# Three accumulator banks, one side bank, and a quarter of each unit's gram parts moved from ScalarE to VectorE

## What is computed

```
dots = jnp.einsum('bfd,bgd->bfg', bottom_output, bottom_output)
x = concatenate([bottom_mlp_output, dots[:, _TRIL_I, _TRIL_J], pad], axis=1)
for w, b in ((w0, b0), (w1, b1), (w2, b2), (w3, b3)):      # 480-1024-1024-512-256
    x = relu(x @ w.T + b)
return x @ w_out.T + b_out
```

## Time and profile before

| | |
|---|---|
| median of 3 runs | 526.17 us (526.14 to 526.34) |
| the profiled execution | 524.71 us, of which the span of instructions is 522.9 us |
| granted TensorE clock over the span | 0.994 |
| TensorE busy | 496.2 us, 95% of the span |
| ScalarE, VectorE, GpSimd busy | 333.8, 289.3, 258.4 us |

### The profile page before, as it was taken

The page is one execution under the profiler, slowest core; times in us unless marked ns, Lnnn a source line. Parts: engine busy times, 40 slices in busy tenths (PEclk is TensorE's granted clock), DMA queues, the critical chain, the costliest instruction groups (busy, mean ns, idle before and its releaser), DMA issues.

```text
span 522.9 us, 13445 instructions
## 1 busy us (share of the span) xinstructions
PE 496.2 (95%) x4073; PEld 485.5 (93%) x4073; DVE 289.3 (55%) x644; ACT 333.8 (64%) x846; POOL 258.4 (49%) x467
## 2 busy tenths in 40 slices
PE   6987988899999999999999999999999999999996
PEld 6976977899999899999999999999999999999996
DVE  2775767476762676357753676356743686231101
ACT  3665788667884698657883698557873798423112
POOL 2710354425774287625764287525763386524221
PEclk9989999999999999999999999999999999999999
DMA  8988877654663666266653657256643762210000
GB/s 229 237 288 169 259 115 121 126 100 72 100 98 69 114 104 107 45 122 112 102 80 78 118 97 112 54 117 106 97 74 88 123 98 37 64 34 1 1 1 0
DMA packets 281054, 53.23 MB, mean 102 GB/s; under 512 B 265126, under 2 KB 279230, under 8 KB 281022
## 3 DMA queue, kind: packets, MB, share of 16 engines
q1 hardware_dynamic: 279090, 52.22, 52.9%
q10 hardware_dynamic: 1932, 0.61, 0.5%
HBM read 45.71 MB, written 7.09 MB: 101 GB/s over the span
## 4 chain that ended last, share of the span: by engine, by line
PE 74%; DMA 7%; ACT 4%; issue 4%; SPq 4%; POOL 3%; DVE 2%; ACTq 0%; POOLq 0%; DVEq 0%
PE acc L732 60%; PE gram_ps L694 7%; DMA rows<-in_r_bottom_output_dram 3%; PE gram_ps L646 2%; DMA early_rows<-in_r_bottom_output_dram 2%; PE gram_ps L675 2%; ACT parts L823 2%; DMA blocks<-grams 2%; SPq L462 2%; ACT h_full L839 1%; SPq L414 1%; POOL parts L568 1%; POOL h_a L583 1%; POOL grams L575 1%; PE turned_ps L651 1%
## 5 line engine op out<-in xcount | busy, mean ns | idle before, releaser
L732 PE MATMUL acc<-h_a,w_hi 128*128 128x256 f32 x1152 | 223.5, 285 | 3.1 <-ACT h_full L839 2.8
L732 PEld LDWEIGHTS acc<-h_a,w_hi 128*128 128x128 f32 x1152 | 184.7, 191 | 5.7 <-ACT h_full L839 3.8
L823 ACT ACTIVATE parts<-gram_ps 27x216 f32<-27x216 f32 x448 | 152.9, 341 | 24.5 <-PE gram_ps L694 14.6
L839 ACT ACTIVATE h_full<-acc,small_t 128x256 f32<-128x256 f32 x172 | 81.4, 473 | 128.9 <-PE acc L732 125.9
L732 PE MATMUL acc<-h_a,w_lo 128*128 128x256 f32 x576 | 158.7, 282 | 0.0
L583 POOL TENSOR_TENSOR h_a<-h_full,h_a 128x256 fp32r<-128x256 f32 x96 | 72.3, 753 | 138.4 <-DVE h_a L956 138.4
L732 PEld LDWEIGHTS acc<-h_a,w_lo 128*128 128x128 f32 x576 | 110.2, 191 | 0.0
L732 PE MATMUL acc<-h_b,w_hi 128*128 128x256 f32 x512 | 97.4, 285 | 0.0
L732 PE MATMUL acc<-x,w_hi 128*128 128x256 f32 x480 | 95.1, 287 | 2.4 <-ACT h_full L839 1.3
L925 DVE STREAM_TRANSPOSE raw<-rows 128x512 f32<-128x512 f32 x112 | 78.7, 703 | 11.6 <-DMA rows<-in_r_bottom_output_dram 11.6
L583 POOL TENSOR_TENSOR h_b<-h_full,h_b 128x256 fp32r<-128x256 f32 x64 | 47.3, 739 | 74.6 <-DVE h_b L956 74.6
(11 more groups left out here) (59 smaller groups left out, 437.9 us busy)
## 6 DMA issues: line engine op xcount, KB each, us to landing
rows<-in_r_bottom_output_dram SPq DMA_DIRECT2D x444, 64.0 KB, 2.0
blocks<-grams SPq DMA_DIRECT2D x30, 216.0 KB, 4.0
w_raw<-in_L_rec_w_dram SPq DMA_DIRECT2D x6, 1024.0 KB, 7.9
early_rows<-in_r_bottom_output_dram SPq DMA_DIRECT2D x12, 224.0 KB, 6.3
stage_pairs<-in_L_rec_w_dram SPq DMA_DIRECT2D x1, 1408.0 KB, 10.2
w_raw<-in_L_rec_w_dram SPq DMA_DIRECT2D x2, 512.0 KB, 9.6
mlp_rows<-r_bottom_mlp_output_dram SPq DMA_DIRECT2D x8, 128.0 KB, 2.2
pairs<-blocks SPq DMA_DIRECT2D x8, 126.0 KB
```

The costliest lines, as they stand in the source:

```text
L732: last = nc.tensor.matmul(acc_slot(c, slot), weight(wp, layer, m, k), in_tile(layer, k, xp), start=(k == 0 and n == 0), stop=(k == K_TILES ...
L823: last = nc.scalar.activation(parts[quad_of(s), u % 2, :, :, 0:FEATS], gram_found(u, s), ACT.Copy)
L839: nc.scalar.activation(h_full[:, slot % 2, :], acc_slot(c, slot), ACT.Relu, bias=small_t[:, slot:slot + 1]).then_inc(drained, 1)
```

## The change

There are now three accumulators (`RING_OF`: slot modulo 3, but slot 21 goes to bank 1), one side bank `side_ps` and the four of `gram_ps`. The side bank holds the dense input in columns 0 to 255 and the output row in the others; the rows turned at the start use it and accumulator 2 in turn. `slot_before` finds the slot whose drain a slot waits for. Only four tiles get their first input early, so W1's groups have all four banks of `gram_ps`. Of each unit's four quads ScalarE copies three, and VectorE the fourth (`gram_parts_rest`), as its last instruction of a hook; TensorE's next use of the banks, VectorE's transposition and GpSimd's sum wait for both.

```
-ACC_RING, TURN_RING, GRAM_RING = 2, 2, 2
+ACC_RING, GRAM_RING, TURN_RING = 3, 2, 2
+RING_OF = [n % 3 for n in range(SLOTS - 1)] + [1]
+QUADS_BY_ACT = 3
-OUT_HOOK, EARLY_TILES = 2, 6
+OUT_HOOK, EARLY_TILES = 2, 4
+def slot_before(slot, first):
+    def bank(of):
+        return ACC_RING if first and of == ACC_RING else RING_OF[of % SLOTS]
+    for of in range(slot - 1, -1 if first else slot - 1 - SLOTS, -1):
+        if bank(of) == bank(slot):
+            return of
+    return None
...
-            among = EARLY_TILES // 3 if BEFORE_CHUNK <= n < LATE_WEIGHTS else GRAM_RING * GRAM_BANKS
-            return gram_ps[:, n % among, :]
+            return gram_ps[:, n % (GRAM_RING * GRAM_BANKS), :]
...
                 pool.wait_ge(parts_done, n)
+                pool.wait_ge(parts_rest_done, n)
...
-                elif BEFORE_CHUNK <= n < LATE_WEIGHTS:
-                    pe.wait_ge(w_done, max(n - 1, BEFORE_CHUNK))
...
                     pe.wait_ge(parts_done, (d - 1) * UNITS + u + 1 - GRAM_RING)
+                    pe.wait_ge(parts_rest_done, (d - 1) * UNITS + u + 1 - GRAM_RING)
...
-                        of = slot - EARLY_TILES if isinstance(c, int) and c == 0 and slot < M_TILES[0] else slot - ACC_RING
+                    of = slot_before(slot, isinstance(c, int) and c == 0)
+                    if of is not None:
                         pe.wait_ge(drained, slot_count(c, of))
...
-                for s in range(GROUP):
+                for s in range(QUADS_BY_ACT):
                     last = nc.scalar.activation(parts[quad_of(s), u % 2, :, :, 0:FEATS], gram_found(u, s), ACT.Copy)
...
+            def gram_parts_rest(d, u):
+                dve.wait_ge(gram_done, d * UNITS + u + 1)
...
+                    dve.wait_ge(grams_done, d * UNITS + u - 1)
+                for s in range(QUADS_BY_ACT, GROUP):
+                    last = nc.vector.tensor_copy(parts[quad_of(s), u % 2, :, :, 0:FEATS], gram_found(u, s))
+                last.then_inc(parts_rest_done, 1)
...
                 dve.wait_ge(parts_done, n)
+                dve.wait_ge(parts_rest_done, n)
```

More of the change, by code:

```diff
@@ L52 @@
 LAST_LAYER = [(0, 0, 3, HIGH), (1, 0, 3, HIGH), (0, 3, 4, HIGH), (1, 3, 4, HIGH), (0, 0, 4, LOW), (1, 0, 4, LOW)]
-ACC_RING, TURN_RING, GRAM_RING = 2, 2, 2
+ACC_RING, GRAM_RING, TURN_RING = 3, 2, 2
 GRAM_BANKS = 2
 XT_RING, XT_LAG = 4, 2
-assert ACC_RING + TURN_RING + GRAM_RING * GRAM_BANKS == 8 and SLOTS % ACC_RING == 0
+assert ACC_RING + 1 + GRAM_RING * GRAM_BANKS == 8
+RING_OF = [n % 3 for n in range(SLOTS - 1)] + [1]
 HOOK, FIRST_HOOK = 18, 6
@@ L274, in dlrm_program @@
         acc = ctx.enter_context(nc.psum_tensor("acc", [P, ACC_RING, 512], F32))
-        turned_ps = ctx.enter_context(nc.psum_tensor("turned_ps", [P, TURN_RING, 512], F32))
+        side_ps = ctx.enter_context(nc.psum_tensor("side_ps", [P, 512], F32))
         gram_ps = ctx.enter_context(nc.psum_tensor("gram_ps", [P, GRAM_RING * GRAM_BANKS, 512], F32))
@@ L302, in dlrm_program @@
         parts_done = sem("parts_done")
+        parts_rest_done = sem("parts_rest_done")
         low_turned = sem("low_turned")
@@ L343, in acc_slot, with turned_bank @@
         def acc_slot(c, slot):
[L344 to L351, removed]
+            if isinstance(c, int) and c == 0 and slot == ACC_RING:
+                return side_ps[:, 0:CHUNK]
+            return acc[:, RING_OF[slot], 0:CHUNK]
+        def turned_bank(u):
+            return side_ps if u % TURN_RING else acc[:, ACC_RING - 1]
+        mlp_bank = side_ps[:, 0:CHUNK]
+        out_bank = side_ps[0:1, CHUNK:]
         def in_tile(layer, k, part):
@@ L392, in turned_cols @@
         def turned_cols(u):
-            return turned_ps[:, u % TURN_RING, 0:UNIT_COLS].rearrange("p (j s f) -> p j s f", s=GROUP, f=FEATS)
+            return turned_bank(u)[:, 0:UNIT_COLS].rearrange("p (j s f) -> p j s f", s=GROUP, f=FEATS)
         def quad_of(s):
@@ L619, in turn_weights @@
                     pe.wait_ge(parts_done, UNITS)
+                    pe.wait_ge(parts_rest_done, UNITS)
                 elif n >= LATE_WEIGHTS + ring:
@@ L650, in turn_rows @@
                 for j in range(UNIT_GROUPS):
-                    last = nc.tensor.transpose(turned_ps[:, u % TURN_RING, j * GROUP_ROWS:(j + 1) * GROUP_ROWS],
+                    last = nc.tensor.transpose(turned_bank(u)[:, j * GROUP_ROWS:(j + 1) * GROUP_ROWS],
                                                src[0:GROUP_ROWS, j, :], ident[0:GROUP_ROWS, 0:GROUP_ROWS])
@@ L715, in products @@
                         pe.wait_ge(w_done, W0_GROUPS if layer == 0 and m >= 4 else groups_for(layer, m))
-                    if not (isinstance(c, int) and c == 0 and slot < EARLY_TILES):
-                        of = slot - EARLY_TILES if isinstance(c, int) and c == 0 and slot < M_TILES[0] else slot - ACC_RING
+                    of = slot_before(slot, isinstance(c, int) and c == 0)
+                    if of is not None:
                         pe.wait_ge(drained, slot_count(c, of))
@@ L940, in early_rest @@
                 last.then_inc(grams_done, 1)
+            def gram_parts_rest(d, u):
+                dve.wait_ge(gram_done, d * UNITS + u + 1)
+                if isinstance(d, int) and d == 1 and u < 2:
+                    dve.wait_ge(parts_zeroed, 1)
+                else:
+                    dve.wait_ge(grams_done, d * UNITS + u - 1)
+                for s in range(QUADS_BY_ACT, GROUP):
+                    last = nc.vector.tensor_copy(parts[quad_of(s), u % 2, :, :, 0:FEATS], gram_found(u, s))
+                last.then_inc(parts_rest_done, 1)
             def turn_low(d, u):
@@ L999, in chunk @@
                         turned_lo(c + step[1], step[2])
+                    elif step[0] == "gram":
+                        gram_parts_rest(c + step[1], step[2])
                     elif step[0] == "sum":
```

## The result

The changed kernel takes 518.76 us in the median of 5 runs (517.22 to 520.58), the kernel before 526.24 beside it. The ratio is 0.9868, 95% interval 0.9846 to 0.989: faster by 6.9 us, 5.8 to 8.1. The profiled execution took 517.22 us (span 515.2, against 522.9).

What follows compares the result with a forecast made beforehand. TensorE, busy for 95% of the span, was taken as the bound, so only its gaps could be won. The terms 3.3 + 1.5 - 1.4 + 0.3 = 3.7 us gave a median of 522.5 us, range 519.8 to 525.0.

Steps and rivals of the forecast that it cites:

- Part 1, the edges: At seven chunk edges, the third accumulator removes slot 0's drain wait: 3.3 us won.
- Part 2, slot 21: Slot 21's wait stays but shrinks with one ScalarE copy fewer, in five chunks: 1.5 us won, between 0.7 and 1.7.
- Part 3: Fourth quad's copy on VectorE delays slot 7's rounding at layer 0's end, in six chunks: 1.4 us lost.
- 253.85 - 0.05 (an earlier start, since ScalarE is ahead): Before slot 7's rounding, VectorE's chain without the copies would end only 0.05 us sooner than 253.85.
- ScalarE's saving is no help there: At layer 0's end, ScalarE's lighter load does not offset VectorE's two added copies; TensorE's gap grows by 0.23 us.
- 0.23 later: Slot 7's rounding would begin at 254.74 instead of 254.51, TensorE going on at 255.09 instead of 254.86.
- a sign of being wrong: The wait for VectorE's rounding at layer 1's first tile gone, meaning the copy is hidden.
- Part 4, chunk 0: Four banks for W1's groups give a lead, paid back at SyncE's row loads; 0.3 us won remains.
- three units' copies on ScalarE, 1.0 us sooner: Before W2's first group, three units' ScalarE copies come last, each 0.34 shorter: 1.0 us sooner, minus 0.72 of moved work.
- VectorE hides the copy: Rival: the copy is as short as on ScalarE, or not held; sum 4.4 to 5.1, 521.1 to 521.8; chance 0.12.
- The third rival: The copy on VectorE is dearer but not ruinous, 0.48 to 0.6 us: 523.8 to 525.1; chance 0.08.
- VectorE becomes the late engine: Rival: a copy of 0.69 us makes VectorE late at the chain and in chunk 0: 528.0, slower; chance 0.08.

Runs made afterwards that it cites:

- the banks alone: The changed kernel with ScalarE copying all four quads of each unit again: 523.88 us, ratio 0.9961.
- the gather first: The changed kernel with SyncE waiting for the pairs' gather to land before loading W1's last quarter: 518.66 us, ratio 0.9881.
- Half the rows: The changed kernel with two of four row loads left out for chunk 1's units 4 to 15 (features wrong): 516.88 us, ratio 0.9838.
- the quad alone: The kernel before with only the fourth quad's copy moved to VectorE, banks as they were: 520.31 us, ratio 0.9896.

## Why the prediction was half right

**Part 1, the edges: right.** Forecast 3.3. In the trace of after the gap is gone at all seven edges. The kernel with the banks alone has 0.51 a chunk, the 0.50 that was read, seven times 3.6, of which 2.0 us (0.8 to 3.3 by its interval) reached the median. In its profiled execution the difference lies in chunk 0: chunk 1's first new unit came 2.6 us later than before (126.91 instead of 124.27), and after a stand of 1.85 us before 98.11 TensorE had a granted clock of 0.66 between 99 and 104 us (1.00 before). Why the clock fell there and not in the changed kernel is open.

**Part 2, slot 21: right, a little small.** The wait shrank from 0.56 to 0.20 us idle, 0.36 in each of five chunks: 1.8 us where 1.5 was taken and 1.7 called the most. The worry about VectorE's copy ahead of the next rounding did not come true.

**Part 3: the step that failed, and nearly all of the miss.** The copy's length (0.40 taken, 0.39 measured), that it is held by its neighbours, and the 0.94 us that the two add to the chain were right: 9.52 - 0.34 - 0.22 + 0.94 + 3.57, the old length of the chain, is 13.47, and 13.48 was measured. Wrong was the step "253.85 - 0.05 (an earlier start, since ScalarE is ahead)" and the sentence "ScalarE's saving is no help there". The start moved by 0.34, and a subtraction of 0.96 became 0.74. This second part is not ScalarE's doing: the subtraction ended 0.46 us after one of GpSimd's both times (253.62 after 253.16, 249.70 after 249.23), so 0.22 us of it were a wait for GpSimd inside VectorE's chain, and the first copy took their place. Both together, 0.51 us beyond the 0.05 assumed, turned "0.23 later" into 0.27 sooner, and six times over a loss of 1.4 into a gain of 1.6: 3.0 of the 3.7 us. The wait for the rounding is gone in the trace of after (250.80), which the forecast itself had named as a sign of being wrong. The rows for it were in the trace of before and were not read: the head of the chain at 249.57, 0.79 long. The forecast cut the chain at an instruction without idle time ahead of it and took its start as VectorE's own. That TensorE's wait for the fourth quad is covered held in the loop; in chunk 0, where a hook comes after 6 matmuls, TensorE waited four times for it, 3.6 us in all, where it had waited four times for ScalarE's copies, 2.7 us, and twice for VectorE's subtraction, 1.3 us.

**Part 4, chunk 0: right in kind.** The lead was paid back at the row loads: the gather first shows it in the trace, and two banks for W1 agree in the time. Half the rows agrees in the length of the stretch, with a gain in time that is not clear of noise. Forecast 0.3; in the profiled pair the stretch up to chunk 1's first new unit (124.27 and 122.97) is 1.3 shorter, 0.4 of it the first edge, so 0.9. Of the parts of that term, "three units' copies on ScalarE, 1.0 us sooner" is near what the quad alone showed (97.34 to 96.24); from the last unit's transposition to that group it is 6.97 us there instead of 7.67, 0.7 of the 1.1. That the pairs' third tile would not have landed was allowed for ("0 to 2.8") and cost nothing in the end.

**Sum.** 3.3 + 1.8 + 1.6 + 0.9 is 7.6; the profiled pair differs by 7.5 (524.71 and 517.22), the medians by 7.5. Of the rivals, "VectorE hides the copy" came nearest, but it was not enough: even at no cost for the copy it gave 5.1, since it left out the 0.29 us at each of six roundings that the earlier drain takes away. The third rival's times come out at 523.4 to 524.9 by the pricing of part 3 (copies of 0.48 and 0.6 us), not at 523.8 to 525.1; nothing hangs on it. "VectorE becomes the late engine" is true of the second copy.

## What to carry to other kernels

When a chain of back-to-back instructions ends in a wait, follow its head back through the other engines, and take an instruction longer than its usual length (0.79 for 0.29) as a wait in disguise: a saving on any engine of that path can arrive at its end, as far as no other engine is later (of 0.69 us here 0.35 did). Moving work to another engine costs next to nothing as long as a gap on that path takes it in, and its full length from the next piece on: 6.9 us won here by the whole change, 10 lost by one more quad. A lead ahead of a queue that paces itself is paid back.

## What was not expected of the hardware

- VectorE's rounding from SBUF to SBUF (0.29 us alone) lasted 0.79 and 0.45 us where it began during one of GpSimd's subtractions, ending 0.15 us after it both times. VectorE's subtraction of two SBUF operands (128x432) took between 0.56 and 1.12 us.
- A lower granted clock between 45 and 50 us came in most variants: 0.76 in the changed kernel and 0.72 with half the rows, where TensorE stood 2.4 and 2.9 us for the pairs, but also 0.54 with two banks for W1, where it stood 0.8 to 1.0 us at a time. With the gather first it came between 65 and 72 us instead (0.53), around the stand of 6.12 us. In these places it did not show in the total, since the rows pace the stretch behind. It is not free everywhere: of the twelve executions with the banks alone, the five with a mean clock of 0.993 or more have a median of 523.12 us, the seven with 0.990 or less 524.36.
- The same kernel's executions spread by 3 us (517.2 to 520.6) where those first shown of the kernel before spread by 0.2; later ones of the kernel before spread as much (523.6 to 527.6 for all but one of 24), so it is not the change's.
